# Straight-line programs in place of hardware loops, and an earlier third low half, in a DLRM tower with a compressed interaction network

## The reference

```python
e = stack([tbl_f[ids[:, f]] for f in range(39)], axis=1)   # (1024, 39, 16)
x0 = xk = e
for W in (f0, f1, f2):                       # (39*39,128), (128*39,128), (128*39,128)
    z = einsum('bfd,bgd->bfgd', x0, xk).reshape(b, 39 * g, d)
    xk = einsum('bpd,pm->bmd', z, W); outs.append(xk)
z = sum(concatenate(outs, axis=1), axis=-1)  # (1024, 384)
h = concatenate([z, dense_ctx], axis=1)
h = relu(h @ W_top1 + b_top1); h = relu(h @ W_top2 + b_top2)
y = h @ W_top3                               # (1024, 1)
```

## Time and profile before

| | us |
|---|---|
| median of 3 runs | 1340.23 |
| lowest and highest | 1337.1, 1341.92 |
| the profiled execution's own time | 1339.86 |
| its span, first to last instruction | 1337.7 |

### The profile page before, as it was taken

The page is one execution under the profiler, slowest core; times in us unless marked ns, Lnnn a source line. Parts: engine busy times, 40 slices in busy tenths (PEclk is TensorE's granted clock), DMA queues, the critical chain, the costliest instruction groups (busy, mean ns, idle before and its releaser), DMA issues.

```text
span 1337.7 us, 25407 instructions
## 1 busy us (share of the span) xinstructions
PE 1261.2 (94%) x5493; PEld 964.8 (72%) x5493; DVE 1056.4 (79%) x3346; ACT 748.6 (56%) x2422; POOL 952.3 (71%) x844
## 2 busy tenths in 40 slices
PE   0799999999999999999999999999999999999999
PEld 0477777777777778677777777777777777877765
DVE  3589996889869997799868998599886898698840
ACT  4356664656546665566645566366654666566641
POOL 6378885788858886688866888578875788666540
PEclk9999999999999999999999999999999999999999
DMA  7532221122222212122211222112221222111000
GB/s 169 151 107 66 66 68 44 42 62 60 59 63 58 57 50 53 47 65 66 66 37 41 60 63 64 51 45 57 64 59 55 66 65 58 43 44 52 3 0 1
DMA packets 121771, 78.48 MB, mean 59 GB/s; under 512 B 77437, under 2 KB 89827, under 8 KB 121653
## 3 DMA queue, kind: packets, MB, share of 16 engines
q1 hardware_dynamic: 106124, 73.45, 19.4%
q0 software_dynamic: 10240, 2.64, 2.3%
q10 hardware_dynamic: 5288, 1.32, 0.5%
HBM read 18.50 MB, written 2.63 MB: 16 GB/s over the span
## 4 chain that ended last, share of the span: by engine, by line
PE 72%; issue 9%; POOL 9%; DVE 5%; ACT 2%; DMA 2%; SPq 1%; POOLq 0%; DVEq 0%; ACTq 0%
PE ps L492 17%; PE ps L496 16%; PE ps L493 16%; PE ps L472 12%; POOL terms L410 6%; PE ps L517 4%; PE ps L508 3%; DVE terms L816 3%; DVE prods_low L788 2%; POOL x_in L386 2%; PE ps L574 2%; ACT terms L661 2%; PE ps L584 1%; DMA w<-in_f 1%; DMA dense_rows<-in_dense_ctx 1%
## 5 line engine op out<-in xcount | busy, mean ns | idle before, releaser
L816 DVE SCALAR_TENSOR_TENSOR terms<-ps,x_scal,terms 128x128 f32<-128x128 f32 x2944 | 807.2, 343 | 192.3 <-ACT terms L661 87.5
L661 ACT ACTIVATE terms<-ps,x_scal 128x128 f32<-128x128 f32 x2048 | 582.9, 368 | 417.3 <-PE ps L496 373.6
L410 POOL TENSOR_TENSOR terms<-terms 128x1024 f32<-128x1024 f32 (+2 forms) x384 | 581.7, 1515 | 217.3 <-DVE terms L816 186.3
L492 PE MATMUL ps<-w_high,x_high 128*128 128x512 f32 (+1 forms) x1280 | 577.2, 451 | 10.7 <-ACT terms L661 7.3
L496 PE MATMUL ps<-w_high,x_low 128*128 128x512 f32 (+1 forms) x1280 | 497.3, 388 | 0.0
L493 PE MATMUL ps<-w_low,x_high 128*128 128x512 f32 (+1 forms) x1280 | 495.7, 387 | 0.0
L386 POOL DMA_INDIRECT x_in<-in_tables,row_at x320 | 305.6, 955 | 89.0 <-issue 85.5
L492 PEld LDWEIGHTS ps<-w_high,x_high 128*128 128x128 f32 x1280 | 241.8, 189 | 92.0 <-issue 28.7
L493 PEld LDWEIGHTS ps<-w_low,x_high 128*128 128x128 f32 x1280 | 242.3, 189 | 76.3 <-issue 29.8
L496 PEld LDWEIGHTS ps<-w_high,x_low 128*128 128x128 f32 x1280 | 241.3, 189 | 51.0
L472 PE MATMUL ps<-prods,w 117*128 117x512 f32 x262 | 135.4, 602 | 13.4 <-issue 13.4
(11 more groups left out here) (48 smaller groups left out, 380.1 us busy)
## 6 DMA issues: line engine op xcount, KB each, us to landing
prods<-x_cols SPq DMA_DIRECT2D x190, 234.0 KB
x_cols<-x_rows SPq DMA_DIRECT2D x93, 78.0 KB
x_first<-x_cols SPq DMA_DIRECT2D x93, 78.0 KB
x_in<-in_tables,row_at POOLq DMA_INDIRECT x320
x_diag<-x_scal SPq DMA_DIRECT2D x256, 9.8 KB
s<-in_f SPq DMA_DIRECT2D x3, 832.0 KB
x_rows<-x_in SPq DMA_DIRECT2D x31, 80.0 KB
wt<-in_W_top SPq DMA_DIRECT2D x1, 768.0 KB
```

The lines of the kernel that those rows point to most:

```text
L410: nc.gpsimd.tensor_tensor(t[:, 0:n], t[:, 0:n], t[:, n:2 * n], ALU.add).then_inc(s_tree, 1)
L492: nc.tensor.matmul(y, x1_high[:, par, at:at + P], high, start=True, stop=False)
L661: op = nc.scalar.activation(terms[:, u % 2, FB * ACT_BANKS.index(q) + i, :], ps[:, (BANKS * u + q) % RING, i * G:(i + 1) * G], ACT.Copy, s ...
L816: nc.vector.scalar_tensor_tensor(out=acc, in0=y, scalar=x0, in1=acc, op0=ALU.mult, op1=ALU.add).then_inc(s_mac, 1)
```

## The change

All hardware loops become Python loops, so that each engine's program is one straight line with constants for semaphore targets and slices. Two entries of the tables move: the low half of the third split chunk (chunk 3) goes from behind bank 2 of tile 2 to behind bank 9 of tile 1 on DVE, and the chunk itself from behind bank 5 to behind bank 6 of tile 2 on PE.

```diff
-LOWS = ((0, 7), (1, 5), (2, 2))
-CIN1 = ((0, 6), (1, 1), (1, 8), (2, 5), (2, 9), (3, 2), (3, 4))
+LOWS = ((0, 7), (1, 5), (1, 9))
+CIN1 = ((0, 6), (1, 1), (1, 8), (2, 6), (2, 9), (3, 2), (3, 4))
...
             for u in range(2):
                 step(0, u, False)
-            with eng.Fori(0, NBATCH - 1) as bt:
+            for bt in range(NBATCH - 1):
                 for u in range(2, STEPS + 2):
                     step(bt, u, False)
...
-            with sp.Fori(1, NBATCH - 1) as bt:
+            for bt in range(1, NBATCH - 1):
                 load_ids(bt + 1)
...
-            with pool.Fori(0, NBATCH - 1) as bt:
+            for bt in range(NBATCH - 1):
                 for u in range(STEPS):
...
-                nc.scalar.activation(r2[:, bass.ds(bt * BATCH, BATCH)], s3[:, F, :], ACT.Copy).then_inc(s_r, 1)
+                nc.scalar.activation(r2[:, bt * BATCH:(bt + 1) * BATCH], s3[:, F, :], ACT.Copy).then_inc(s_r, 1)
```

More of the change, by code:

```diff
@@ L679, in store_r @@
                 act.wait_ge(s_s3e, bt * STEPS + STEPS + CREDIT_S3E)
-                nc.scalar.activation(r2[:, bass.ds(bt * BATCH, BATCH)], s3[:, F, :], ACT.Copy).then_inc(s_r, 1)
+                nc.scalar.activation(r2[:, bt * BATCH:(bt + 1) * BATCH], s3[:, F, :], ACT.Copy).then_inc(s_r, 1)
                 act.wait_ge(s_l3, bt + 1)
-                nc.scalar.activation(r3[:, bass.ds(bt * BATCH, BATCH)], ps[:, S3_BANK, R3_AT:R3_AT + BATCH],
+                nc.scalar.activation(r3[:, bt * BATCH:(bt + 1) * BATCH], ps[:, S3_BANK, R3_AT:R3_AT + BATCH],
                                      ACT.Copy).then_inc(s_r, 1)
@@ L795, in split_x1 @@
                                         x1_high[:, j % 2, :].bitcast(F32), ALU.subtract).then_inc(s_x1l, 1)
-                nc.vector.tensor_reduce(r1[:, bass.ds(gf * (GCOLS // D), GCOLS // D)],
+                nc.vector.tensor_reduce(r1[:, gf * (GCOLS // D):(gf + 1) * (GCOLS // D)],
                                         ps[:, X1_BANK, :].rearrange("p (b d) -> p b d", d=D),
```

## The result

The changed kernel takes 1291.66 us (median of 4, 1290.09 to 1292.17) against 1339.16 for the one before: ratio 0.964, 95% interval 0.962 to 0.966. The forecast was 1291. In the profiled executions the span fell from 1337.7 to 1288.3, by 49.4 us; the sum of the prediction was 49.0. By the medians it is 47.5 us.

A forecast was written before the change was run, and what follows sets the result against it. The prediction took PE's work plus PE's holes as the bound. Savings of 34.0 + 1.3 + 1.3 + 12.4 = 49.0 us from 1339.86 gave 1290.9, stated as 1291, with a range of 1286 to 1307.

The forecast's parts named there:

- (a'): At PE's entry into its hardware loop: 1.15 us of idle and the restart go, 1.3 us.
- (a): Loop returns and late chunk 3: removing both saves 34.0 us in batches 1 to 6, 1.3 in batch 0.
- (b): At chunk 3 behind the layer-2 sum: a wait counted as busy time, 0.4 us per group, 12.4 us in all.
- (c): On DVE: the low half, moved before bank 1's and 2's macs, fits a 0.54 us idle gap and costs nothing.
- (d): On PE: chunk 3 one bank later delays SP's copy of the next group's fourth factor by 0.7 us, costing nothing.
- (e): On all queues: registers, branches and dynamic slices go, but PE's pace is the same either way, so nothing more is gained.
- (f): Instruction loading: straight code makes PE walk 128 tile steps instead of code for 32; taken as zero cost.
- 1 (POOL as the bound): POOL, late after renumbering, costs PE 1 to 1.5 us a batch, seven times: 1300 us; chance 0.10.
- 2 (the tree first): POOL's add beats the low half, PE waits at bank 6: 1.5 x 31 = 46 us, 1337; chance 0.05.
- 3 (PE starved): PE waits for instructions: about 34 more blocks at 1.65 us each, 56 us, 1347; chance 0.03.
- 4 (block borders on ACT and DVE): Chunk 3's holes close, but straight ACT and DVE queues stall as long as the returns did: 1306 us; chance 0.05.

The follow-up runs named there:

- e7: The kernel before the change, with POOL's tree adds cut to 8 of 128 columns; 1318.05 us, ratio 0.986.
- e1: The kernel before the change with its hardware loops kept and only the two table entries moved; 1300.48 us, ratio 0.972.
- e2: The kernel before the change with all loops made straight and the old table entries kept; 1306.91 us, ratio 0.976.
- e10: As e8, but PE loops over the batches while all other engines are straight; 1285.06 us, ratio 0.960.
- e5: The changed kernel with chunk 3 back behind bank 5 of tile 2, so only the low half moved; 1289.50 us, ratio 0.965.
- e11: As e2 (straight, old tables), but POOL alone loops over the batches; 1316.28 us, ratio 0.985.
- e8: The changed kernel with PE's wait for the layer-3 weights moved 16 tile steps later, to the first layer-3 part; 1284.90 us, ratio 0.960.
- e4: The changed kernel (new tables) with only ACT looping over the batches and all other engines straight; 1299.76 us, ratio 0.971.
- e9: The changed kernel with the third low half behind bank 1 of tile 2, inside POOL's tree; 1301.22 us, ratio 0.972.
- e3: The changed kernel (new tables) with only ACT straight and all other engines looping; 1291.08 us, ratio 0.965.
- e12: As e8, with chunk 3 back behind bank 5 and ACT's first-group copies issued behind the sixth layer-2 weight piece; 1286.48 us, ratio 0.961.

## Why the prediction was right, and where it was right by luck

The total and its mechanism, holes on PE that close, were right; the working held less well than the sum. Part of the match is luck: the profiled execution of before, from which the sum started, had a late start that no other profile shows (a'), and the profiled execution after was the quickest of its four. By the medians the gain is 47.5 us, 1.5 less than the sum.

(a) *Holes that go: 34.0 + 1.3 us forecast.* Batches 1 to 6 and the end of batch 0 gave what was said: 43.4 against 34.0 + 9.6 with (b), and 2.4 against 1.3 + 1.2. The reason is that batch 7 was the right sample. The split of it was wrong. I gave the returns 6 x 2.1 = 12.6 us and put the waits of the first groups under chunk 3's lock. e7 shows that these 1.4 us belong to ACT's return, and the returns cost 21.0 us of the 34.0. Since moving the low half closes these waits too (e1: 1.55 a return is left), the two edits are not additive, and e1 and e2 each came out 5.5 and 18 us faster than I expected from that split.

(a') *PE's entry into its loop: 1.3 us.* This step failed. e10: the entry is free. The hole was the load's, and it grew to 4.9 us. That 2.4 us were gained ahead of the second group all the same is luck of the sample: the profiled run of before had a late start. DVE idled 1.5 to 2.3 us before each of its last three pieces of the layer-2 weights, the load of the layer-3 weights was issued at 56.0 us (53.4 in the changed kernel), and PE reached the last bank of the first tile at 59.35 us. In the other thirteen profiles that is 51.7 to 55.6, also in e1 and e7, whose start is the program of before (53.5 and 53.0). e1 ends its first group at 85.27, the changed kernel at 84.89. So nearly all of the 2.4 us is that one execution, and what delayed it stays open.

(b) *0.4 us a group of hidden wait: 12.4 us.* Right: groups went from 35.64 and 35.67 to 35.29, 0.35 to 0.4 each, and e5 shows that it was a wait and not the chunk's place.

(c) *Low half at no cost in DVE's gap.* Right: the eight macs of banks 1 and 2 start 2.66 us after PE begins tile 1's last bank, 2.69 before, and the idle of 0.54 or 0.36 became 0.26 or none.

(d) *The chunk's move at no cost.* Right, and it was not needed (e5).

(e) *Loops' register work gives nothing more.* Wrong, by its own argument: I looked at PE's pace alone. e11: on POOL, with the old tables, the loop costs 7.7 us in six batches. It didn't show in the sum, because the moved low half no longer cares when the tree runs.

(f) *Instruction blocks: nothing.* Right: 44 blocks, no hole, and e10 against e8 is 0.16 us. The Trainium skill (Runtime: NRT & Kernel Launch, "Instruction fetch mechanics") says that fetching in sequence is mostly hidden, and that a taken branch out of the pages held stalls until its target is fetched. The first agrees with PE's 44 blocks. The second agrees with ACT's return, which comes with 15 more packets (e4), and with PE's, which is free and whose queue brings only 12 blocks in the whole span (e10); that the fetch is what ACT waits for is not shown.

*Rivals.* 1 (POOL as the bound): groups are 35.28 and 35.29 throughout, also behind the renumbering. The straight code also gave POOL 0.13 us a step (e11) that I had not counted. 2 (the tree first): never, in 31 low halves; DVE was 0.23 us ahead where the two met. e9 puts a locked low half behind the macs of bank 1, not ahead of them, so the 46 us for it were not tested; what e9 measured was 8.6 us in six batches. 3 (PE starved) and 4 (block borders on ACT and DVE): nothing seen.

## What to carry to other kernels

If a kernel's loop has a peeled, straight last round, read that round's period first: it prices the removal of the loop without a guess, but it doesn't say which stall belongs to which cause, and stalls that share a cause must not be added. Put an operation that can be locked out by another engine where that engine is sure to be idle or later, not where its input is just in time. And when the steady state is tight, go through each constant wait at the start: the wait for the layer-3 weights, placed 16 tile steps before their first use, cost 5.5 us here.

## What the runs showed of the hardware that I had not expected

- A loop's return costs the engines very differently: ACT idles 2.65 to 3.49 us behind its last store at the six returns of the kernel before, against 0.40 in its straight last batch and 0.48 in the changed kernel; PE loses nothing (e10). One looping engine brings the whole price (e4). DVE's return makes nothing late either (e3), but DVE idles 3.4 us behind that place with and without a loop, so a price smaller than that would not show.
- The low half, a VectorE operation with two SBUF inputs, shows the lock as a longer duration, not as idle time: 1.56 to 1.92 us instead of 0.68 in batches 1 to 6 of before, up to 3.06 in e9. The macs, with one input in PSUM, are not held: eight of them take 2.16 us while POOL's tree runs (405.26 in the changed kernel) and 2.16 in e7, where the tree is short.
- Five copies issued from ACT's queue between its own operations held it for 6.6 us (e12); three pieces later they left 1.73 us of idle (e8).
